# Flamingo block on one core: later loads for chunks 2 and 3, their statistics and projections one step later, and four small transfers issued by ScalarE

## The reference, cut to what matters

```python
Q = (layernorm(x) @ Wq.T + bq)   # 16 heads of width 8
K = (ctx @ Wk.T + bk)
V = (ctx @ Wv.T + bv)
attn = softmax(Q @ K.T / sqrt(8))
x = x + tanh(g_xattn) * ((attn @ V) @ Wo.T + bo)
z = layernorm(x)
topk_s, topk_i = top_k(softmax(z @ gate_w + gate_b), 2)
for i in range(8):               # wi: the gate's weight of expert i, 0 where it is not chosen
    y = relu(z * wi @ w1[i] + b1[i]) @ w2[i] + b2[i]
    out = where(wi > 0, y, out)
x = x + tanh(g_ffn) * out
```

## Time and profile before

| | us |
|---|---|
| median of 3 runs | 174.5 (173.58 to 177.56) |
| the profiled execution's own time | 172.94 |
| its span, first to last instruction | 171.1 |
| outside of the span | 1.84 |

### The profile page before, as it was taken

One profiled execution on the slowest core, in us unless ns is written; L12 is line 12 of the kernel. 1 busy time (PEld: TensorE's weight loads), 2 busy tenths in 40 slices (PEclk: granted clock), 3 DMA queues, 4 the chain that ended last, 5 costly groups with the idle time before them and its releaser, 6 DMA issues. The chain is left out here.

```text
span 171.1 us, 5192 instructions
## 1 busy us (share of the span) xinstructions
PE 128.8 (75%) x1654; PEld 103.0 (60%) x1655; DVE 122.8 (72%) x437; ACT 94.8 (55%) x236; POOL 89.1 (52%) x153
## 2 busy tenths in 40 slices
PE   7789436899999987768697662007997999999960
PEld 2256434568676865456474441006986999999950
DVE  5578578668986999999997588886425666677520
ACT  3155401667786674457485720434976677777620
POOL 8648717444534433328227703736008886657661
PEclk9999955799999999999969996555899999999996
DMA  5899999033335548794442300114123331010100
GB/s 136 263 316 222 250 215 251 10 98 96 98 99 151 161 121 280 228 343 150 159 130 61 142 14 17 36 52 121 35 74 100 100 99 38 26 44 30 34 0 0
DMA packets 18354, 20.53 MB, mean 120 GB/s; under 512 B 3012, under 2 KB 15815, under 8 KB 18132
## 3 DMA queue, kind: packets, MB, share of 16 engines
q1 hardware_dynamic: 16216, 16.96, 37.1%
q0 software_dynamic: 1248, 2.23, 3.9%
q10 hardware_dynamic: 864, 1.01, 1.9%
HBM read 10.88 MB, written 3.35 MB: 83 GB/s over the span
## 5 line engine op out<-in xcount | busy, mean ns | idle before, releaser
L703 DVE TENSOR_REDUCE smax<-pair 128x8 f32<-128x1024 f32 x32 | 38.6, 1215 | 4.7 <-PE pair L1041 4.4
L547 ACT ACTIVATE probs<-pair 128x1024 f32<-128x1024 f32 x32 | 31.9, 1011 | 5.8 <-PE pair L1053 5.8
L482 POOL DMA_INDIRECT out<-k_stack,token x23 | 23.2, 1010 | 20.5 <-DVE k_stack L923 10.0
L612 ACT ACTIVATE k_stack<-pair,q_stack 128x128 f32<-128x128 f32 x74 | 21.6, 367 | 11.4 <-PE pair L1144 11.4
L1144 PE MATMUL pair<-q_stack 128*128 128x128 f32 x184 | 25.8, 287 | 0.0
L1144 PEld LDWEIGHTS pair<-q_stack 128*128 128x128 f32 x184 | 23.9, 203 | 0.0
L410 POOL DMA_INDIRECT rows_dram<-routed,rowpos x16 | 16.1, 1004 | 13.1 <-DVE rowpos L776 9.7
L416 POOL CAST nmax<-smax 128x16 bf16<-128x16 f32 x16 | 3.1, 196 | 35.7 <-DVE smax L703 35.6
L1084 PE MATMUL bank<-probs,vall 128*18 128x128 f32 x512 | 17.9, 283 | 0.0
L1041 PE MATMUL pair<-k_stack,q_stack 64*128 64x128 bf16 x256 | 13.3, 234 | 5.2 <-issue 2.6
L574 ACT ACTIVATE oT<-bank 128x256 f32<-128x256 f32 x16 | 6.2, 386 | 14.8 <-PE bank L1092 13.1
(11 more groups left out here) (169 smaller groups left out, 263.1 us busy)
## 6 DMA issues: line engine op xcount, KB each, us to landing
wexp<-in_wexp SPq DMA_DIRECT2D x8, 514.0 KB, 4.0
k_stack<-k_part SPq DMA_DIRECT2D x24, 128.0 KB, 3.6
q_stack<-q_part SPq DMA_DIRECT2D x24, 128.0 KB, 3.3
q_stack<-rows_dram SPq DMA_DIRECT2D x23, 72.0 KB, 1.9
x<-in_x SPq DMA_DIRECT2D x4, 256.0 KB, 8.0
ctxT<-in_ctxT SPq DMA_DIRECT2D x3, 256.0 KB, 9.4
q_stack<-in_zeros SPq DMA_DIRECT2D x6, 128.0 KB, 3.4
rows_dram<-late_pack SPq DMA_DIRECT2D x1, 576.0 KB, 5.1
```

Of the source, the lines that this page charges most:

```text
L482: pool.indirect_dma_start(io["out"], bass.IndirectOffsetOnAxis(ap=token[:, t:t + 1].bitcast(u32), axis=0), result[t], None, bounds_check=T ...
L547: A(probs[s % 2][:, t].rearrange("p h g q -> p (h g q)"), pairs[home["shifted", s, t]][:, :], ACT.Exp, scale=HD ** -0.5).then_inc(s_exp, 1)
L612: ins = A(hidT[t % R][:, c, :], bank[1 + t % 2][:, c * P:(c + 1) * P], ACT.Relu, bias=w1cur[t % R][:, HID + c:HID + c + 1])
L703: V.reduce_max(smax[q % 2][:, :, CHUNK * t:CHUNK * (t + 1)], pairs[home["score", q, t]][:, :].rearrange("p (h g k) -> p h g k", h=2, g=CHU ...
```

## The change

- SP issues the loads of x and context of chunk 2 only after the fills of chunk 0, and those of chunk 3 after the row of maxima of sequence 2.
- The two middle-part fills of chunk 0's Q are issued by ScalarE, between `middle("q")` and `high("k", 1)`; so are the rows of maxima of sequences 0 and 1.
- `first_stats(2)` and `first_stats(3)` leave the stretch before the loop and stand in steps 1 and 5, between the two maxima. `FRONT_K`, `FRONT_Q`, `FRONT_G` (projections, their remainders on VectorE, the gate's product) move by one step. GpSimd's `powers`, `normalise(3)`, `add_bias(1)` follow.
- The table `later` moves by about one entry. Chunk 2 now has the lower parts of both stacks in entry 5; chunk 3's Q lower parts stand in entry 10 instead of 9, padding in 11.
- In steps 1 and 2 PE does five filler products (`keep_warm(5)`) and then `scores(n, 1)` ahead of the transposition of the maxima.

The diff; of `later` the three lines of each side stand whole:

```diff
@@ -230,7 +230,9 @@
         ALL_STACK = 16 * TERMS
         LAG_MT, LAG_S2, LAG_PV, LAG_HT = 1, 3, 4, 5
         STEPS = SEQS + LAG_HT
-        FRONT_K, FRONT_Q, FRONT_G = {2: 2, 6: 3}, {3: 2, 7: 3}, {4: 2, 8: 3}
+        FRONT_K, FRONT_Q, FRONT_G = {3: 2, 7: 3}, {4: 2, 8: 3}, {5: 2, 9: 3}
+        FRONT_S = {1: 2, 5: 3}
+        ACT_ROWS = 2
         CHOOSE, WEIGH, PLACE = {10: 0, 14: 1}, {11: 0, 15: 1}, {11: 0, 15: 1, 19: 2}
 
         def items(n):
@@ -309,17 +311,20 @@
             load_x(0)
             load_x(1)
             load_ctx(1)
-            for c in range(2, CHUNKS):
-                load_x(c)
-                load_ctx(c)
             sp.wait_ge(s_clear["k"], 1)
             sp.dma_start(kst[6:P:32, 0].rearrange("r g t -> r (g t)"), io["minus"][0:2 * HD:4, :]).then_inc(s_slots[0], 16)
             sp.wait_ge(s_clear["q"], 1)
-            for c in range(2):
-                for n in "kq":
-                    fill(n, c, 0)
-                    fill_lower(n, c)
-                slots(c + 1)
+            fill("k", 0, 0)
+            fill_lower("k", 0)
+            fill("q", 0, 0)
+            fill("q", 0, 2)
+            load_x(2)
+            load_ctx(2)
+            slots(1)
+            for n in "kq":
+                fill(n, 1, 0)
+                fill_lower(n, 1)
+            slots(2)
 
             def padding():
                 sp.dma_start(b2g[:, :, :].rearrange("p e d -> p (e d)"), io["b2"].to_broadcast([P, EXPERTS * D])).then_inc(s_b2, 16)
@@ -328,10 +333,10 @@
                 sp.dma_start(fronts, spare.unsqueeze(1).to_broadcast([P, EXPERTS, RW])).then_inc(s_spare, 16)
                 sp.dma_start(rows_dram[EXPERTS * CAP:EXPERTS * CAP + P, :], spare).then_inc(s_spare, 16)
 
-            later = {2: lambda: fill("k", 2, 0), 3: lambda: fill("q", 2, 0), 4: lambda: fill_lower("k", 2),
-                     5: lambda: fill_lower("q", 2), 6: lambda: (fill("k", 3, 0), slots(3)), 7: lambda: fill("q", 3, 0),
-                     8: lambda: fill_lower("k", 3), 9: lambda: fill_lower("q", 3), 10: padding}
-            for m in range(SEQS):
+            later = {2: lambda: (load_x(3), load_ctx(3)), 3: lambda: fill("k", 2, 0), 4: lambda: fill("q", 2, 0),
+                     5: lambda: (fill_lower("k", 2), fill_lower("q", 2)), 6: lambda: slots(3), 7: lambda: fill("k", 3, 0),
+                     8: lambda: fill("q", 3, 0), 9: lambda: fill_lower("k", 3), 10: lambda: fill_lower("q", 3), 11: padding}
+            for m in range(ACT_ROWS, SEQS):
                 c, u = seq_of(m)
                 sp.wait_ge(s_mtc, m + 1)
                 sp.dma_start(qst[6:P:32, c, :, u], nmaxT[m % 2][:, :]).then_inc(s_mrow[m % 4], 16)
@@ -426,10 +431,9 @@
             powers(1)
             normalise(1)
             lower_parts("k", 1)
-            powers(2)
             lower_parts("q", 1)
             split_max(0)
-            powers(3)
+            powers(2)
             split_max(1)
             normalise(2)
             split_max(2)
@@ -439,10 +443,11 @@
             split_max(4)
             lower_parts("q", 2)
             split_max(5)
+            powers(3)
+            split_max(6)
             normalise(3)
-            split_max(6)
+            split_max(7)
             add_bias(1)
-            split_max(7)
             lower_parts("k", 3)
             split_max(8)
             lower_parts("q", 3)
@@ -527,6 +532,10 @@
             turn_out(0)
             high("q", 0)
             middle("q")
+            act.wait_ge(s_mid["q"], 1)
+            for s in range(TERMS):
+                if TERM_PARTS["q"][s] == 1:
+                    act.dma_start(qst[s:P:SLOTS, 0], part["q"][0][:, 1, :]).then_inc(s_stack["q"][0], 16)
             high("k", 1)
             act.wait_ge(s_vzero, 1)
             values(0)
@@ -577,6 +586,10 @@
                     A(headsT[:, :], heads_turned, ACT.Identity, bias=bv).then_inc(s_htc, 1)
                 if m is not None:
                     copy_max(m)
+                if m is not None and m < ACT_ROWS:
+                    c, u = seq_of(m)
+                    act.wait_ge(s_mtc, m + 1)
+                    act.dma_start(qst[6:P:32, c, :, u], nmaxT[m % 2][:, :]).then_inc(s_mrow[m % 4], 16)
                 if s is not None and n < SEQS:
                     exponent(s, 1)
                 if n in FRONT_K:
@@ -680,10 +693,8 @@
             take_rest("q", 0)
             low_part("q")
             take_rest("k", 1)
-            first_stats(2)
             dve.wait_ge(s_late, 16)
             V.tensor_copy(routed[:, :, TOKEN_AT].bitcast(i32), token_no.bitcast(i32))
-            first_stats(3)
             take_rest("q", 1)
             dve.wait_ge(s_gox, 1)
             V.tensor_copy(wog, bank[1][:, 8:16])
@@ -853,6 +864,8 @@
                     weigh(WEIGH[n])
                 if 0 <= n - LAG_HT - 1 < SEQS:
                     moments(n - LAG_HT - 1)
+                if n in FRONT_S:
+                    first_stats(FRONT_S[n])
                 if q is not None:
                     maxima(q, 1)
                 if 0 <= n - LAG_HT - 1 < SEQS:
@@ -1069,6 +1082,11 @@
                         shifted_scores(s, 1)
                 if q is not None:
                     scores(q, 0)
+                if 0 < n < LAG_S2:
+                    pe.wait_ge(s_vc, 2)
+                    pe.wait_ge(s_xg, 2)
+                    keep_warm(5)
+                    scores(q, 1)
                 if m is not None or v is not None or h is not None:
                     if n == LAG_MT:
                         pe.wait_ge(s_azero, 1)
@@ -1092,7 +1110,7 @@
                     T(heads_turned, heads_out[:, :, :, :].rearrange("p j r d -> p (j r d)"), ident).then_inc(s_ht, 1)
                 if s is not None and n < SEQS:
                     shifted_scores(s, 1)
-                if q is not None:
+                if q is not None and not 0 < n < LAG_S2:
                     scores(q, 1)
                 if n in FRONT_K:
                     c = FRONT_K[n]
```

## The result

The changed kernel is slower: 183.69 us median of 4 runs (183.56 to 183.76) against 176.03 us for the kernel before (4 runs, 173.58 to 178.31), ratio 1.055, 95% interval 1.051 to 1.060. Most kernels have some executions that are more than 1.5% longer than their fastest, and the ratios leave these out while the medians do not. I had said 178.0, at most 181.0. The profiled execution took 183.56 us with a span of 181.7, 10.6 more than before.

What follows compares the result with a forecast made beforehand. VectorE's instruction list was taken to bound the attention loop. Terms -1.4 + 2.8 - 0.9 + 1.8 + 1.9 = +4.2 gave 177.1 us on the profiled time and 178.7 on the median; forecast 178.0, range 173.5 to 181.0.

Steps and rivals of the forecast that it cites:

- The start: Before the loop: first scores at 20.3 instead of 21.7 us, set by PE's list, -1.4 us.
- The statistics: Steps 1 and 5: two statistics calls between VectorE's maxima, 1.4 us each, nothing covering them, +2.8 us.
- Waits of VectorE in steps 0 to 7: First half of the loop: VectorE's waits fall from 5.1 to 4.2 us, -0.9 us.
- The K projection at the full clock takes 1.13 instead of 2.07, so the 1.50 falls to about 0.5: Chunk 2's K projection: faster PE shortens VectorE's wait before the K remainder from 1.50 to about 0.5 us.
- the 0.95 and 0.5 that I had: Steps 3 and 4: VectorE waits 0.95 us behind GpSimd's normalising of chunk 2, then about 0.5.
- Chunk 2's fills: Step 8: fills 1.0 us late for (8, 0), 0.7 to 0.8 more at (8, 1), +1.8 us.
- Chunk 3's fills: Step 12: fills 1.2 us late for (12, 0), 0.7 more at (12, 1), +1.9 us.
- the 0.7 in front of (12, 1): Step 12: VectorE waits 0.7 us more for the second scores because PE's lead is missing.
- a low clock at step 12 as a rival: Step 12: PE's rest for the fill drops its clock, 2.5 us more, 179.6 to 181.2 us; chance 0.12.
- The tail: After the last maxima: the last stretch is a chain that shifts whole, 0 us.
- The rival with the fills in time: Steps 8 and 12: no late fills, only start, statistics and waits count, +0.5, 173.4 to 175.0 us; chance 0.25.
- the one that is not slower: Steps 0 to 4: PE's full clock feeds VectorE without holes, no late fills, -1.3, 171.6 to 173.2 us; chance 0.18.

Runs made afterwards that it cites:

- e9: The changed kernel run once more, unaltered, as the measure for its chip; 181.56 us (2 runs).
- e15: The e13 kernel with only the two middle fills of chunk 0's Q issued by ScalarE instead of SP; 171.85 us, 0.986 of the kernel before.
- e13: The e11 kernel unaltered, run again on another chip; 170.21 us, 0.976 of the kernel before.
- e6: The kernel before with only the statistics of chunks 2 and 3 moved into steps 1 and 5; 179.98 us, 1.029 of the kernel before.
- e11: The e10 kernel plus, in steps 1 and 2, five fillers and scores (n, 1) ahead of the transposition; 170.19 us, 0.978 of the kernel before.
- e10: The kernel before with context loads of chunks 2 and 3 behind chunk 0's fills and rows of maxima 0 and 1 issued by ScalarE; 173.77 us, 0.996.
- e1: The changed kernel with the transfer table mended for chunks 2 and 3, fills one entry earlier; 182.67 us, 1.006 of the kernel before.
- e14: The e13 kernel with projections of chunks 2 and 3 one step later, GpSimd's list and fill table as in e12; 173.96 us, 0.991 of the kernel before.
- e12: The changed kernel with the table of e1, x loaded early and the statistics ahead of the loop; 176.18 us, 1.015 of the kernel before.
- e4: The changed kernel with 7 filler products on PE ahead of scores (8, 0) and 16 ahead of (12, 0); 185.34 us, no ratio.
- e3: The changed kernel with only chunk 3's table entries mended; 182.61 us, 1.025 of the kernel before.
- e2: The changed kernel with only chunk 2's table entries mended; 184.38 us, no ratio.

## Why the prediction was wrong

I compare with the changed kernel's second execution, e9, whose span of 178.2 is 7.1 over before, near the 7.7 by which the medians differ.

- **The start, -1.4:** measured -1.15 in the first profile and -1.6 in e9; the first scores came at 20.77 and 20.37, where I had 20.3. PE's list, not the stack, set it, as I had it. My 0.61 for an issue was a slip: 3.77/6 is 0.63. ScalarE's two issues took 1.31 us, and in e15 they moved the start by 0.8 against e13, taken from the K projection of chunk 0 (5.88 and 6.28) to (0, 0) (20.71 and 21.92); I had 0.7. The Trainium skill (DMA: Bandwidth & Descriptors, "Issuing engines are not separate DMA queues") says that a second issuing engine saves only the time of issuing; the runs agree: e15 gained nothing from it. What it gave SP was worth nothing, and what it took from ScalarE was on the path.
- **The statistics, +2.8:** right; 24.69 to 26.08 and 42.80 to 44.19, and e6 alone +2.8.
- **Waits of VectorE in steps 0 to 7, -0.9: this term failed.** Two effects of the change are in it. The order of steps 1 and 2 gave -1.8 (33.65 in e11 against 35.44 before and 35.51 in e10). The projections one step later cost +2.1 (e1 less the statistics, 38.48 - 2.78 - 33.65; in e14 2.9, of which 0.79 are waits at step 8), so the term is +0.3. The step that broke is "The K projection at the full clock takes 1.13 instead of 2.07, so the 1.50 falls to about 0.5". It took 2.07, and the wait was 1.76, in e9 1.49; in e12, where it took 1.12, the wait was 0.71. The waits of step 3 (1.34 in e9) and step 4 (1.02) were also longer than the 0.95 and 0.5 that I had. The sum was wrong besides: the waits that I listed for after add up to 4.65 and not 4.2, the 0.5 of step 5 being left out. That wait did not show in e9, but I gave no reason for leaving it out, so that this came right by luck.

  `powers(2)` now waits on GpSimd for the statistics of step 1 and stands ahead of `split_max(1)`; so PE rested 2.27 us in front of the transposition at 28.68, and its clock stood at half from 29.3 us on. I had looked at the clock only behind the start. That this rest lowered the clock isn't shown: in e14 the statistics stand ahead of the loop, the longest rest there is 1.48 us, and the projection took 2.08 all the same. GpSimd's row of the changed kernel, the first of `powers(2)`:

```profile
26.25 1.01 POOL L377 TENSOR_TENSOR rstd<-veps,power 128x4 f32<-128x4 f32 x1 [2.05 <-DVE veps L666]
```

- **Chunk 2's fills, +1.8:** in e9 against e1 +1.7, right. In the first profile it was +3.5. There PE's clock fell too, at 56.6 us, the wait in front of (8, 1) was 1.03 for 0.36 and that of the Q remainder 2.17 for 1.35.
- **Chunk 3's fills, +1.9: this term was undersized.** It measured +3.2 and +3.4. The part for (12, 0) was near, 1.39 and 1.44 for my 1.2. What failed is the 0.7 in front of (12, 1), which took PE's work between the two scores at the full clock: it measured 1.81 and 1.55, and 0.36 in e4, where the clock was full. PE was at half clock there, and the V products took 1.91 for 1.07. With the full clock the fills cost 1.6 by e4, near the term; the half clock adds 1.6 to 1.8.

  I had a low clock at step 12 as a rival with a chance of 0.12 and 2.5 us, in place of the forecast, and my reason for it was wrong as well. I had it fall in the rest for the fills. In the changed kernel it fell at 73.7, 1.2 us ahead of that rest, in e9 at 70.2, 2.9 ahead, and in e1 and e3, whose fills are in time there, at 70.0 and 70.9. In e2 it fell within the rest, at 72.7. So the rest for the fills isn't what lowers the clock at step 12; without it the clock falls there as well. But the late fills took the lead from PE that makes a half clock cost nothing in e1 and e3, and while PE rested the clock stayed low: it was at half until 83.9 in the changed kernel and 80.5 in e9, but back at 75.4 with the fillers of e4. What lowers it there stays open.

  The Trainium skill (TensorE: Matmul & The Clock Gate, "HAM oscillation — how this bites in real kernels") describes waits for DMA in which the clock falls, so that the work behind them starts slow. The trace agrees on the slow work, 1.91 us for 1.07 after the wait, but not on the fall, which came first.
- **The tail, 0:** 84.61 and 83.39 against 82.88. A wait of VectorE in it was 1.86 before, 1.85 in e9 and e11, but 2.81 in the changed kernel, 2.79 in e13 and 2.87 in e1. It comes and goes in executions of the same kernel and isn't the change's.

The sum of e9: -1.6 + 2.8 + 0.3 + 1.7 + 3.2 + 0.7 (from (13, 0) on) = 7.1. The misses are 1.2 in the waits, 1.3 at step 12, 0.7 behind it. The first profile's 10.6 holds 3.5 more: 1.8 up to (9, 0), nearly all at step 8, 1.1 behind (13, 0), 0.4 at the start and 0.2 at step 12. The rival with the fills in time and the one that is not slower are out. The one with the low clock named a cost that came, but for another reason, and its 179.6 to 181.2 was also too low.

## What to carry to other kernels

When a forecast says that PE will wait and lose its lead, price two things: the wait, and PE's work behind it at half clock, since nothing hides a slow PE any more. A work item that lies in an engine's idle time (statistics before the loop, a projection in a step in which PE rests) can cost its whole length, and its waits, where it is put instead; here both did. Test the parts of a many-part change alone: here three parts (late context loads, rows of maxima issued by ScalarE, scores ahead of the transposition) make a kernel 2.2 to 2.4% faster than before (intervals 1.6 to 3.1%), and the others hide it. An earlier start is worth something only when what the pipeline needs next, here a row of 8 KB, isn't queued behind large transfers.

## What the runs showed that was not expected

- Near the same length of rest the clock did one or the other. PE rested 1.83 us ahead of scores (8, 0) in e9 and then did the V product in 1.07 us; it rested 1.77 us in e12 and then took 1.91. This one fall cost e12 a wait of 1.80 in front of (8, 1), where e9 had 0.36. First e9, then e12:

```profile
54.72 0.40 PE L1054 MATMUL pair<-k_stack,q_stack 64*128 64x128 bf16 x8 [1.83 <-issue]
55.05 1.07 PE L1102 MATMUL bank<-probs,vall 128*18 128x128 f32 x32
```

```profile
53.42 0.40 PE L1054 MATMUL pair<-k_stack,q_stack 64*128 64x128 bf16 x8 [1.77 <-issue]
53.75 1.91 PE L1102 MATMUL bank<-probs,vall 128*18 128x128 f32 x32
```

  In e3 a rest of 2.03 us at the same place left the clock at 1.0 as well. So the length of that rest alone doesn't decide it here; what does stays open.
- The mended table of e1 isn't enough in e12, where the waits at step 8 are back. A likely reason is that with the statistics out of step 5 VectorE and PE come to (8, 0) sooner, so that a cost that was removed had been covering another. But e14 has that table too, with the statistics out of step 5, and waits 0.43; in e12 3.56 us also passed from the end of the last fill's issue to the scores, against 2.87 in e9. How much is which isn't shown.
- SP needed 3.23 us for three fills that took 1.92 at the same place in e9: the third issue took 1.94 us instead of 0.6, in the stretch that decides step 8. The lower K fills of chunk 2 show the same in e1, e12 and e14 (2.93 to 3.06 us). What holds an issue up isn't shown.
- The kernel before spreads over 173 to 178 us on a chip. Part of it is in the first load: PE's first K projection began between 5.64 (e9) and 7.80 us (e12) on the same chip, waiting for the context of chunk 0, and everything behind it shifts. It is why starts are compared within a profile here.
